# Splitting the product with C in a selective scan between VectorE and GpSimd, in two batches of four

## The chip, the cores and the metric

The kernel runs on one core of one Trainium2 chip. The time is the device time of one execution in microseconds (us): 928.15 us is the median of three runs of the kernel before (926.04, 928.15 and 931.03). Smaller is better.

## The reference, cut to what matters

Two decoder layers run over x (4 batches, 256 tokens, 256 features). The change lies in the first block of the second layer, a selective scan with 512 inner features and 16 states:

```python
def step(h, inputs):              # over the 256 tokens
    dA_t, dBu_t, C_t = inputs
    h = h * dA_t + dBu_t
    y = jnp.einsum('bdn,bn->bd', h, C_t)
    return (h, y)
```

dA is exp(delta * A), dBu is delta * B * u, and y sums, over the 16 states, the state times its value of C at that token. Around it stand, in each batch, linear attention, cross attention and a mixture of experts (layer 0), and after it a cross attention with 32 heads and a second mixture of experts (layer 1).

## The kernel before, in words

**Tiles.** Features lie on the 128 partitions and tokens along the row. A step n of the scan (n from 0 to 15) holds two of the four feature tiles (i = 0, 1) and two states (s = 0, 1), so its state is 128 x 2 x 512 numbers: for each i a half of 512, made of two quarters of 256 tokens, one for each s. The states of five steps lie in a ring (`state(n)`). In the first and the last batch (`alone(b)`) steps 0 to 7 take feature tiles 0 and 1 with all 16 states, and steps 8 to 15 tiles 2 and 3. The middle batches go through the steps in another order.

**One step.** GpSimd multiplies delta*u by B into the state's place (`scan_input`, L603, two steps ahead). ScalarE writes exp(delta*A) into the PSUM banks F[0] and F[1] (`scan_decay`, L846), each after the scan of the step before has read that bank. VectorE runs two scans of 512 (L1606), one for each i. TensorE copies the row of C to all partitions in the PSUM bank F[2] (`spread_c`, two bf16 matmuls against `bcp` and `pick`), after VectorE's product of the step before has read that bank. VectorE multiplies the whole state by F[2] (L1616, 128x1024; in the last step two products of 512, L1613). TensorE adds the quarters into a PSUM bank for y by matmuls with the identity (`sum_states`, L1011). For an even step it adds all four quarters. For an odd step below 15 GpSimd first adds the two quarters of each half (`pair_sum`, L613), and TensorE adds the two results (`parts = 1`). The trace counts each fp32 matmul as two instructions.

**Order.** Every engine is a queue that runs in the order written. The order is a fixed merge of two streams of phases, F (layer 0 and the scan) and B (layer 1 after the scan), by the tables `FILL` and `LATER`. Phase `s{n}` holds step n. In batch 0 its scan (from 138.5 us to 213.9 us) is interleaved with the cross attention and the layer 0 experts of batch 1; in batch 3 (673.4 us to 757.2 us) with the 32-head attention and then the layer 1 experts of batch 2. Inside phase `s{n}` TensorE does `spread_c(n)`, then `sum_states(n-2)`; GpSimd does `scan_input(n+2)`, then the sum of quarters of n-1 if that is odd; ScalarE does `scan_decay(n+1)`; VectorE does scans and product of n. Between them come the other stream's phases: ScalarE's Silu of layer 0 experts (L788), with a load of its table before and another load before the next exponential, its exponentials of the attention (L887) and its Tanh of layer 1 experts (L908); VectorE's L1540, L1693, L1745 and L1751.

The functions that the change touches:

Of the kernel before, what the change touches and what calls it, by code (L numbers as in the profile page):

```python
# [19 lines left out]
ALU = mybir.AluOpType  # L20
# [3 lines left out]
P = 128  # L24
B, S, D = 4, 256, 256
# [10 lines left out]
NSTEP = 2 * NK  # L36
# [188 lines left out]
def build(nc, ins, out, known):  # L225
    ctx = ExitStack()
    with ctx:  # L227
        def sb(name, shape, dt=F32):
            return ctx.enter_context(nc.sbuf_tensor(name, shape, dt))
# [76 lines left out]

        cs = du[:, :, :].rearrange("p d t -> p (d t)")[:, 0:C_END]
        bcp = sb("bcp", [P, S], BF16)

        arena = sb("arena", [P, 8192 + 2560])  # L310
        A_RING = 8
# [41 lines left out]
        F = [banks_f[:, 512 * i:512 * i + 512] for i in range(4)]  # L353
# [5 lines left out]
        def place(b):  # L359
            return places[b]  # L360
# [22 lines left out]
        pf, af, df, gf, pb, ab, db, gb = (steps[n] for n in names)  # L383
# [29 lines left out]
        def head(n):  # L413

            q, j = divmod(n, 4)
            return 8 * (q // 2) + 2 * j + q % 2
# [22 lines left out]

            return NK * dp + NK - 1 if alone(b) else NSTEP - 2 + dp  # L440

        def in_halves(n):

            return n % 2 == 1 and n < NSTEP - 1

        def state(n):

            r = n % RING
            if r == 4:
                return hb5  # L450
            return hb[:, r, :, :]
# [14 lines left out]
        def later(b):  # L466
            return b > 0

        def alone(b):
            return b in (0, B - 1)  # L470
# [84 lines left out]
        def _(pool):  # L555
            g = nc.gpsimd
# [24 lines left out]
            def rsqrt(dst, src, wait, steps_, name):  # L581
                pool.wait_ge(*wait)
                g.tensor_tensor(dst, src, minus_half[:, 0:src.shape[-1]], ALU.pow).then_inc(steps_.step(name), 1)  # L583
# [25 lines left out]
            def pair_sum(b, n):  # L609

                pool.wait_ge(*df.at(f"hc{n}", b))
                h = state(n)
                g.tensor_tensor(h[:, :, 0:S], h[:, :, 0:S], h[:, :, S:2 * S], ALU.add)\  # L613
                    .then_inc(gf.step(f"half{n}"), 1)
# [31 lines left out]
            def front(b, ph):  # L646
                pl = place(b)
                if ph in PAIRS:
                    n = 2 * PAIRS.index(ph) + 1
                    h = head(n)  # L650
                    if n in (1, 9) and not later(b):
                        pool.wait_ge(init_v, 2 if n == 1 else 5)
                    pool.wait_ge(*af.at(f"c{n}", b))
                    a_ = pl.att[:, n % A_RING, :]
                    g.tensor_tensor(a_[:, 0:S], a_[:, 0:S], decay[:, h, :], ALU.mult).then_inc(gf.step(), 1)  # L655
                    g.tensor_tensor(a_[:, S:S + P], a_[:, S:S + P], decay[:, h, 0:P], ALU.mult)\
                        .then_inc(gf.step(f"a{n}"), 1)
                if ph == "ob":
                    rsqrt(rs[:, :], ve[:, :], df.at("ve_o", b), gf, "rs_o")
                    rsqrt(rs[:, :], ve[:, :], df.at("ve_ln1", b), gf, "rs_ln1")  # L660
                if ph == "xc":
                    rsqrt(rs[:, :], ve[:, :], df.at("ve_sim", b), gf, "rs_sim")
                if ph == "xd":
                    rsqrt(rs[:, :], ve[:, :], df.at("ve_ln2", b), gf, "rs_ln2")
                if ph == "fd3":
                    rsqrt(rs3[:, :], ve3[:, :], df.at("ve_ln3", b), gf, "rs_ln3")
                if ph == "m3" and not later(b):
                    prepare(b, gf)
                if ph == "d4":
                    scan_input(b, 0)  # L670
                    scan_input(b, 1)
                if ph in STEPS:
                    n = STEPS.index(ph)
                    if n + 2 < NSTEP:
                        scan_input(b, n + 2)
                    if n >= 1 and in_halves(n - 1):
                        pair_sum(b, n - 1)
                if ph == "u2":
                    rsqrt(rsu[:, :], veu[:, :], df.at("ve_ln4", b), gf, "rs_ln4")

# [31 lines left out]
        def _(act):  # L712
# [122 lines left out]
            def scan_decay(b, n):  # L835

                k, dp = part(b, n)
                if k == 0:
                    act.wait_ge(*af.at(f"delta{dp}", b))
                for i in range(2):  # L840
                    if n >= 1:
                        act.wait_ge(*df.at(f"scan{n - 1}_{i}", b))
                    d = 2 * dp + i
                    for s in range(2):
                        j = d * NS + 2 * k + s
                        ins_ = a.activation(two(F[i][:, :])[:, s, 1:S], delta[:, d, 1:S], ACT.Exp, scale=a_neg[:, j:j + 1])  # L846
                    ins_.then_inc(af.step(f"dA{n}_{i}"), 1)

            def back(b, ph):
                bk = home(b)  # L850
# [64 lines left out]
        def _(pe):  # L915
# [68 lines left out]
            def sum_states(b, n):  # L984

                k, dp = part(b, n)
                if n == 0:
                    pe.wait_ge(*af.at("delta0", b))
                if n == 0 and not alone(b):
                    pe.wait_ge(*db.at("x4_read", b - 1))  # L990
                if n < NSTEP - 1:
                    pe.wait_ge(*(gf.at(f"half{n}", b) if in_halves(n) else df.at(f"hc{n}", b)))
                parts = 1 if in_halves(n) else 2
                if alone(b) and n == NK:
                    pe.wait_ge(*df.at("y_read0", b))
                if n < NTURN and not alone(b):
                    for t in range(TT):
                        for i in range(2):
                            for s in range(parts):
                                c, d = s * S + t * P, (2 * dp + i) * P  # L1000
                                last = t_.matmul(y_bank(b, t)[:, d:d + P], state(n)[:, i, c:c + P], ident[:, :],
                                                 start=(n == 0 and i == 0 and s == 0),
                                                 stop=(n >= NTURN - 2 and s == parts - 1),
                                                 is_transpose=True, skip_group_check=True)
                    last.then_inc(pf.step(f"y{n}"), 1)
                    return
                for i in range(2):
                    if n == NSTEP - 1:
                        pe.wait_ge(*df.at(f"hc{n}_{i}", b))
                    for s in range(parts):  # L1010
                        last = mm(y_bank(b, dp)[:, i * S:i * S + S], ident[:, :], state(n)[:, i, s * S:s * S + S],  # L1011
                                  alone(b) and k == 0 and i == 0 and s == 0, k == NK - 1 and s == parts - 1)
                last.then_inc(pf.step(f"y{n}"), 1)
# [345 lines left out]
        def _(dve):  # L1359
            v = nc.vector  # L1360
# [67 lines left out]
            def front(b, ph):  # L1428
# [12 lines left out]
                if ph in PAIRS:  # L1441
                    n = 2 * PAIRS.index(ph)
                    h = head(n)
# [119 lines left out]
                if ph == "m4":  # L1563

                    for i in range(2):
                        dve.wait_ge(*af.at(f"tap{i}", b))
                        for j in range(1, NCONV):
                            if j > 1:
                                own(df, b)
                            for d in (2 * i, 2 * i + 1):  # L1570
                                c, w = acc[:, S * d + j:S * d + S], V_CW + 4 * d + NCONV - 1 - j
# [24 lines left out]
                if ph in STEPS:  # L1596
                    n = STEPS.index(ph)
                    for i in range(2):
                        h = state(n)[:, i, :]
                        dve.wait_ge(*af.at(f"dA{n}_{i}", b))  # L1600
                        if n == 0:
                            dve.wait_ge(*df.at("first", b))
                            dve.wait_ge(*gf.at(f"dbu0_{i}", b))
                        elif i == 0:
                            dve.wait_ge(*gf.at(f"dbu{n}", b))
                        v.tensor_tensor_scan(h, F[i][:, :], h, 0.0, ALU.mult, ALU.add)\  # L1606
                            .then_inc(df.step(f"scan{n}_{i}"), 1)
                    dve.wait_ge(*pf.at(f"c{n if alone(b) else n - n % 2}", b))
                    own(df, b)
                    h = state(n)  # L1610
                    if n == NSTEP - 1:
                        for i in range(2):
                            v.tensor_tensor(h[:, i, :], h[:, i, :], F[2][:, :], ALU.mult)\  # L1613
                                .then_inc(df.step(f"hc{n}_{i}"), 1)
                    else:
                        v.tensor_tensor(h, h, F[2][:, :].unsqueeze(1).to_broadcast([P, 2, 2 * S]), ALU.mult)\  # L1616
                            .then_inc(df.step(f"hc{n}"), 1)
                    if alone(b) and n == NK + 1:
                        gated_output(b, 0)
# [250 lines left out]
```

## Time and profile before

| what | us |
|---|---|
| median of 3 runs | 928.15 |
| lowest, highest | 926.04, 931.03 |
| the profiled execution, its own time | 930.76 |
| its span in the trace | 929.0 |
| TensorE busy | 840.1 |
| VectorE busy | 636.2 |
| ScalarE busy | 368.0 |
| GpSimd busy | 349.4 |

The profile is of one execution. A group of rows gives, for one line of the kernel, the busy time in all and the mean time of one instruction. PE is the matmul, PEld the weight load beside it, DVE is VectorE, ACT is ScalarE, POOL is GpSimd. A span of time is told in us from the span's start. The granted clock of TensorE is a share of full speed (2.4 GHz), 0.5 being the lower level (1.2 GHz).

### The profile page before, as it was taken

Reading aid. Unit: us, or ns where it says so; the run is one execution under the profiler, and the core shown is the slowest. Engines: PE = TensorE matmul, PEld = TensorE weight load, DVE = VectorE, ACT = ScalarE, POOL = GpSimd, SP = SyncE. Lnnn points to the kernel's source line nnn. Section 1 sums busy time; section 2 is a strip of 40 time slices with the busy share of each in tenths; the row PEclk is TensorE's granted clock in tenths of the full one; section 3 lists DMA queues with packets and bytes.
Section 4 is the critical chain, followed back from the end, with each engine's and each line's share of the span. In section 5 each row is a group of like instructions: output and inputs, shape, how many; then the busy total and the mean of one; then the engine's idle time right before and its main releaser. Section 6 shows DMA issues by size and latency. Waiting matters only on the chain. (4 is left out here: it accounts for less than half of the span.)

```text
span 929.0 us, 12411 instructions
## 1 busy us (share of the span) xinstructions
PE 840.1 (90%) x4566; PEld 632.2 (68%) x4590; DVE 636.2 (68%) x1218; ACT 368.0 (40%) x741; POOL 349.4 (38%) x337
## 2 busy tenths in 40 slices
PE   6889986878988999997989999998697999999996
PEld 5677765647635778886636888876134888738885
DVE  5342479898946278998955469998989886625222
ACT  5121365752254354442263354445385323171110
POOL 4300446651303038781301229861547622102221
PEclk9999998999988999999999999999789899999999
DMA  7202050022030054441020044432100124313442
GB/s 232 93 21 83 11 195 1 0 86 102 1 114 1 22 173 152 135 138 46 2 113 1 7 153 139 135 102 84 56 1 1 40 68 132 103 35 123 161 142 74
DMA packets 26927, 76.10 MB, mean 82 GB/s; under 512 B 3436, under 2 KB 5420, under 8 KB 26228
## 3 DMA queue, kind: packets, MB, share of 16 engines
q1 hardware_dynamic: 26612, 75.26, 24.5%
q8 instruction: 36, 0.59, 0.3%
q14 instruction: 23, 0.19, 0.1%
q10 hardware_dynamic: 256, 0.07, 0.0%
HBM read 74.13 MB, written 1.11 MB: 81 GB/s over the span
## 5 line engine op out<-in xcount | busy, mean ns | idle before, releaser
L919 PE MATMUL B<-late 128*128 128x256 f32 (+2 forms) x1064 | 243.5, 382 | 2.0 <-POOL late L702 1.5
L919 PEld LDWEIGHTS B<-late 128*128 128x128 f32 (+1 forms) x1064 | 199.2, 193 | 32.9 <-POOL late L702 3.2
L603 POOL TENSOR_TENSOR arena<-du,arena 128x1024 f32<-128x1024 f32 x60 | 141.0, 2362 | 30.9 <-PE F L919 30.4
L1606 DVE TENSOR_TENSOR_SCAN arena<-F,arena 128x512 f32<-128x512 f32 x128 | 149.2, 1207 | 2.9 <-ACT F L846 2.8
L846 ACT ACTIVATE F<-delta,a_neg 128x255 f32<-128x255 f32 x256 | 109.6, 468 | 67.3 <-DVE arena L1606 66.8
L702 POOL TENSOR_TENSOR late<-late 128x512 f32<-128x512 f32 x42 | 53.5, 1274 | 136.0 <-DVE late L1751 105.7
L1616 DVE TENSOR_TENSOR arena<-arena,F 128x1024 f32<-128x1024 f32 x60 | 73.3, 1221 | 8.7 <-PE F L919 3.0
L583 POOL TENSOR_TENSOR rs<-ve,minus_half 128x2 f32<-128x2 f32 (+1 forms) x20 | 15.3, 764 | 162.6 <-DVE ve L1556 71.8
L887 ACT ACTIVATE late<-B 128x512 f32<-128x512 f32 x96 | 51.9, 593 | 23.1 <-PE B L919 18.1
L1682 DVE TENSOR_REDUCE nmx<-B 128x4 f32<-128x1024 f32 x48 | 56.6, 1220 | 3.5 <-PE B L919 3.3
L908 ACT ACTIVATE late<-B 128x512 f32<-128x512 f32 x42 | 24.9, 592 | 85.6 <-PE B L919 84.0
L919 PE MATMUL F<-arena,ident 128*128 128x256 f32 x232 | 57.8, 390 | 0.1
L724 ACT ACTIVATE arena<-F 128x384 f32<-128x384 f32 (+6 forms) x44 | 22.2, 508 | 64.1 <-PE F L919 45.2
L919 PEld LDWEIGHTS F<-arena,ident 128*128 128x128 f32 x232 | 43.3, 198 | 5.9 <-DVE arena L1613 0.5
L919 PE MATMUL F<-arena 128*128 128x256 f32 (+1 forms) x204 | 40.0, 343 | 6.7 <-DVE arena L1439 6.1
L919 PEld LDWEIGHTS F<-arena 128*128 128x128 f32 (+1 forms) x204 | 34.6, 196 | 14.0 <-DVE arena L1439 6.8
L613 POOL TENSOR_TENSOR arena<-arena 128x512 f32<-128x512 f32 x28 | 35.9, 1282 | 19.1 <-DVE arena L1616 19.1
L655 POOL TENSOR_TENSOR arena<-arena,decay 128x256 f32<-128x256 f32 x24 | 18.8, 783 | 58.4 <-ACT arena L724 58.1
L1745 DVE SCALAR_TENSOR_TENSOR late<-late,B 128x512 f32<-128x512 f32 x42 | 28.7, 683 | 16.7 <-ACT late L908 16.0
L919 PE MATMUL B<-late,k_t 128*128 128x512 bf16 x85 | 31.0, 416 | 8.3 <-ACT late L887 5.8
L702 POOL TENSOR_TENSOR late<-arena 128x512 f32<-128x512 f32 x14 | 17.8, 1268 | 50.2 <-DVE arena L1751 44.2
L919 PE MATMUL B<-k_t,late 128*128 128x512 bf16 x89 | 28.5, 419 | 8.4 <-DVE nmx L1682 4.9
(359 smaller groups left out, 1470.2 us busy)
## 6 DMA issues: line engine op xcount, KB each, us to landing
late<-in_w_moe SPq DMA_DIRECT2D x112, 384.0 KB, 3.4
room<-in_w_f SPq DMA_DIRECT2D x4, 2544.0 KB, 9.1
arena<-b_out SPq DMA_DIRECT2D x32, 256.0 KB, 5.5
room<-in_w_l SPq DMA_DIRECT2D x4, 768.0 KB, 6.5
w_m<-in_w_m SPq DMA_DIRECT2D x1, 2112.0 KB
room<-in_w_l SPq DMA_DIRECT2D x4, 512.0 KB, 4.3
x_t<-in_x_t SPq DMA_DIRECT2D x4, 256.0 KB, 2.6
x_tok<-in_x_tok SPq DMA_DIRECT2D x4, 256.0 KB, 5.5
```

The source lines that it names most:

```text
L603: g.tensor_tensor(state(n).rearrange("p d (s t) -> p d s t", s=2), du[:, 2 * dp:2 * dp + 2, :].unsqueeze(2).to_broadcast([P, 2, 2, S]), b_ ...
L613: g.tensor_tensor(h[:, :, 0:S], h[:, :, 0:S], h[:, :, S:2 * S], ALU.add)\
L702: g.tensor_tensor(hid1[:, s:s + 2, :], pair_ring(b, p).rearrange("p (u t) -> p u t", u=2), bk.crs[:, int(2 * p >= MTE), :].unsqueeze(1).to ...
L724: a.activation(dst, src, ACT.Copy, **kw).then_inc(steps_.step(name), 1)
L846: ins_ = a.activation(two(F[i][:, :])[:, s, 1:S], delta[:, d, 1:S], ACT.Exp, scale=a_neg[:, j:j + 1])
L887: a.activation(probs[:, m % 4, :], bk.K[m % 2][:, :], ACT.Exp).then_inc(ab.step(f"p{m}"), 1)
L908: a.activation(pair_ring(b, p), pair_banks(b, p)[0][:, :], ACT.Tanh, scale=0.5)\
L919: return t_.matmul(dst, lhsT, rhs, start=start, stop=stop, skip_group_check=True)
L1606: v.tensor_tensor_scan(h, F[i][:, :], h, 0.0, ALU.mult, ALU.add)\
L1616: v.tensor_tensor(h, h, F[2][:, :].unsqueeze(1).to_broadcast([P, 2, 2 * S]), ALU.mult)\
L1682: v.tensor_reduce(nmx[:, s, g // 4, :, j:j + 2].rearrange("p v i -> p i v"), max_banks(b, n), AX_X, ALU.max, negate=True).then_inc(db.step ...
L1745: v.scalar_tensor_tensor(th, th, 1.0, gates[:, :], ALU.add, ALU.mult)\
```

## The change

In the first and last batch, for the odd steps 1 to 13 (seven in each of the two batches): ScalarE copies F[2] to a new tile `c_copy` in SBUF (128x512) right after it has issued the exponentials of that step. VectorE waits for this copy and multiplies only the half i = 0 by F[2]. GpSimd multiplies the half i = 1 by `c_copy`, after the second scan of the step, in the place in its queue where it had added quarters. TensorE waits for both and adds all four quarters. The middle batches are as they were.

```diff
+        c_copy = sb("c_copy", [P, 2 * S])
...
-        def in_halves(n):
-            return n % 2 == 1 and n < NSTEP - 1
+        def in_halves(b, n):
+            return n % 2 == 1 and n < NSTEP - 1 and not alone(b)
+        def split(b, n):
+            return n % 2 == 1 and n < NSTEP - 1 and alone(b)
...
-                    if n >= 1 and in_halves(n - 1):
+                    if n >= 1 and in_halves(b, n - 1):
                         pair_sum(b, n - 1)
+                    if n >= 1 and split(b, n - 1):
+                        pool.wait_ge(*df.at(f"scan{n - 1}_1", b))
+                        pool.wait_ge(*af.at(f"cc{n - 1}", b))
+                        h = state(n - 1)[:, 1, :]
+                        g.tensor_tensor(h, h, c_copy[:, :], ALU.mult).then_inc(gf.step(f"hp{n - 1}"), 1)
...
                     ins_.then_inc(af.step(f"dA{n}_{i}"), 1)
+                if split(b, n):
+                    act.wait_ge(*pf.at(f"c{n}", b))
+                    if n >= 2:
+                        act.wait_ge(*gf.at(f"hp{n - 2}", b))
+                    copy(c_copy[:, :], F[2][:, :], af, f"cc{n}")
...
-                    pe.wait_ge(*(gf.at(f"half{n}", b) if in_halves(n) else df.at(f"hc{n}", b)))
-                parts = 1 if in_halves(n) else 2
+                    pe.wait_ge(*(gf.at(f"half{n}", b) if in_halves(b, n) else df.at(f"hc{n}", b)))
+                if split(b, n):
+                    pe.wait_ge(*gf.at(f"hp{n}", b))
+                parts = 1 if in_halves(b, n) else 2
...
+                    elif split(b, n):
+                        dve.wait_ge(*af.at(f"cc{n}", b))
+                        v.tensor_tensor(h[:, 0, :], h[:, 0, :], F[2][:, :], ALU.mult).then_inc(df.step(f"hc{n}"), 1)
```

## Rows read from the trace of the kernel before

**Rows 1.** The page, part 1: busy us, share of the span, instructions.
```profile
PE 840.1 (90%) x4566; PEld 632.2 (68%) x4590; DVE 636.2 (68%) x1218; ACT 368.0 (40%) x741; POOL 349.4 (38%) x337
```
**Rows 2.** By stretch: length; PE, PEld, DVE, ACT, POOL busy (instructions); granted clock; DMA.
```profile
138.50:213.90 75.40, 58.50 (x243) 43.77 (x242) 70.72 (x90) 42.68 (x82) 43.75 (x23) 0.91 0.08 27
157.35:164.82 7.47, 6.89 (x34) 5.46 (x33) 7.26 (x8) 6.51 (x13) 6.29 (x4) 1.00 0.01 2
673.40:717.00 43.60, 36.18 (x244) 17.88 (x248) 39.42 (x53) 30.30 (x67) 23.78 (x17) 0.93 0.00 1
717.00:757.20 40.20, 39.75 (x178) 34.01 (x179) 36.05 (x55) 14.62 (x37) 22.69 (x25) 0.89 0.19 60
757.20:916.90 159.70, 158.22 (x848) 122.93 (x854) 72.47 (x143) 39.24 (x72) 31.28 (x26) 1.00 0.35 111
```
**Rows 3.** Groups by shape, 717 to 757.2: count, busy us, mean ns, idle before.
```profile
L1616 DVE TENSOR_TENSOR arena<-arena,F 128x1024 f32<-128x1024 f32 x6 | 7.3, 1222 | 1.6 <-PE F L919 1.1
...
L1613 DVE TENSOR_TENSOR arena<-arena,F 128x512 f32<-128x512 f32 x2 | 1.3, 685 | 0.1
...
L724 ACT ACTIVATE late<-B 128x512 f32<-128x512 f32 x2 | 1.2, 597 | 8.3 <-PE B L930 8.0 <-PE B L919 0.3
```
**Rows 4.** Timeline, batch 0, sums of quarters: start, length, what, idle before.
```profile
157.39 1.03 PE L919 MATMUL F<-arena,ident 128*128 128x256 f32 x4
...
162.17 1.89 PE L919 MATMUL F<-arena,ident 128*128 128x256 f32 x8
```
**Rows 5.** Timeline, batch 0, around the start of step 5's scans.
```profile
163.59 1.67 ACT L846 ACTIVATE F<-delta,a_neg 128x255 f32<-128x255 f32 x4
...
164.64 0.39 PE L919 MATMUL F<-bcp,pick 128*128 128x256 bf16 x2 [0.58 <-DVE arena L1616]
...
164.82 2.33 DVE L1606 TENSOR_TENSOR_SCAN arena<-F,arena 128x512 f32<-128x512 f32 x2
...
166.08 0.87 ACT L846 ACTIVATE F<-delta,a_neg 128x255 f32<-128x255 f32 x2 [0.81 <-DVE arena L1606]
```
**Rows 6.** Timeline of VectorE, batch 0, between steps 7 and 8.
```profile
178.04 0.42 DVE L1540 TENSOR_TENSOR late<-late,B 128x256 f32<-128x256 f32 x1 [2.08 <-ACT late L788]
```
**Rows 7.** Timeline of VectorE: the same two products, at two places.
```profile
186.67 2.52 DVE L1649 TENSOR_TENSOR arena<-arena,sres 128x256 f32<-128x256 f32 x2
...
214.76 0.76 DVE L1649 TENSOR_TENSOR arena<-arena,sres 128x256 f32<-128x256 f32 x2
```
**Rows 8.** Timeline of GpSimd, batch 0, beside the first of these.
```profile
182.83 4.67 POOL L603 TENSOR_TENSOR arena<-du,arena 128x1024 f32<-128x1024 f32 x2 [5.32 <-PE F L919]
187.46 1.45 POOL L613 TENSOR_TENSOR arena<-arena 128x512 f32<-128x512 f32 x1
```
**Rows 9.** Timeline of TensorE, batch 0, behind step 13's sum of 11.
```profile
204.67 1.13 PE L919 MATMUL B<-w_lb,late 72*128 72x256 f32 x4 [1.95 <-ACT late L724]
```
**Rows 10.** Timeline, batch 3, steps 3 and 4, beside the attention of batch 2.
```profile
687.94 2.23 ACT L887 ACTIVATE late<-B 128x512 f32<-128x512 f32 x4
...
688.67 0.79 PE L919 MATMUL B<-late,k_t 128*128 128x512 bf16 x2
...
690.05 1.67 ACT L846 ACTIVATE F<-delta,a_neg 128x255 f32<-128x255 f32 x4
...
691.17 1.21 DVE L1606 TENSOR_TENSOR_SCAN arena<-F,arena 128x512 f32<-128x512 f32 x1
```
**Rows 11.** Timeline, batch 3, step 11, beside the experts of batch 2.
```profile
735.81 0.87 ACT L846 ACTIVATE F<-delta,a_neg 128x255 f32<-128x255 f32 x2 [1.65 <-DVE arena L1606]
...
737.57 0.38 PE L919 MATMUL F<-bcp,pick 128*128 128x256 bf16 x2
...
737.77 0.60 ACT L908 ACTIVATE late<-B 128x512 f32<-128x512 f32 x1
...
737.99 1.22 DVE L1616 TENSOR_TENSOR arena<-arena,F 128x1024 f32<-128x1024 f32 x1 [1.10 <-PE F L919]
...
740.58 0.69 DVE L1751 TENSOR_TENSOR late<-late,B 128x512 f32<-128x512 f32 x1 [0.77 <-PE B L919]
```

## The prediction

> **What bounds the kernel now.** I read the busy line of the page first, then the busy time of each engine in five stretches, then the timelines around single steps. There TensorE stands at 90% of the span and VectorE at 68% [rows 1]: TensorE is the engine that is short on the whole. The change acts in two stretches only, so what counts is what is short there [rows 2]. In batch 0's scan (75.4 us) VectorE is busy 70.7 us and TensorE 58.5: VectorE is the bound, with TensorE idle 17 us. In the first part of batch 3's scan, beside the attention of batch 2 (43.6 us), VectorE has 39.4 and TensorE 36.2. In the second part, beside the experts (40.2 us), TensorE has 39.75: it is the bound, and behind it to the end it has 158.2 of 159.7 us. So a microsecond of TensorE's work added there has no gap to vanish in, and one saved on VectorE there is worth nothing by itself.
>
> **The prices.** For each of the 14 odd steps:
> - VectorE: a product of 1024 (1.22 us) becomes one of 512 (0.685) [rows 3]: -0.54, in all -7.5 us.
> - TensorE: an odd sum of four instructions (1.03 us) becomes one of eight (1.89) [rows 4]: +0.86, in all +12.0 us.
> - ScalarE: a copy of 128x512 from PSUM to SBUF, which the trace shows at 0.597 us [rows 3]: +0.60, in all +8.4 us, and the wait for `c{n}` before it.
> - GpSimd: a product of 128x512 out of SBUF in the place of a sum of the same size (L613, 1.45 us) [rows 8]: 0. The bound from the other side: L603 multiplies twice as many in 2.34 us [rows 8], 1.17 for this size, -0.3 us a step. No one waits for GpSimd in these stretches, since the sum on TensorE stands a phase later.
>
> So it takes 7.5 us from VectorE and gives 12.0 to TensorE. Now where each falls.
>
> **Batch 0, steps 1 to 7 (beside the layer 0 experts of batch 1).** A pair of steps lasts 7.47 us, VectorE has 7.26 of it and TensorE 6.89 [rows 2]. With 0.86 more TensorE has 7.75: it becomes the bound, and the pair grows by 0.28. TensorE's present wait for the product, 0.58 us [rows 5], is smaller than what is added. Two pairs are filled like this (steps 3 and 5): +0.6. Step 1 has less of TensorE's work beside it, and VectorE's gain shows in part, since the exponentials of the next odd step are the other limit: in rows 5 the first two of four are done at 163.59 + 0.83 = 164.42, only 0.4 us ahead of the scan at 164.82. I take -0.2. The copy itself is hidden in steps 3 and 5: ScalarE idles 0.81 us behind the exponentials of step 5, and the copy takes 0.60 of it [rows 5]. In step 7 it isn't hidden: two Silus with their table loads come behind it, and VectorE waits 2.08 us for one of them [rows 6]. There +0.6 for the copy and -0.5 for the scan before it, which comes earlier: +0.1. Sum of steps 1 to 7: +0.5 us.
>
> **Batch 0, steps 9 to 13.** Step 9: behind it stand VectorE's two products L1649, which took 2.52 us there and 0.76 us at 214.76 [rows 7]. Beside the long one GpSimd ran without a gap from 182.83 to 188.91 [rows 8], and VectorE's second product ended right behind it. So VectorE waits there for GpSimd's end, which hangs on TensorE's sums (5.32 us of wait), and a product that ends 0.54 earlier only waits longer: 0. Steps 11 and 13: VectorE is dense, TensorE idles up to 1.95 us [rows 9] and takes the 0.86: -0.54 each, -1.1. Batch 0 in all: 0.5 - 1.1 = -0.6 us. Bounds: if every odd step gained, -3.8; if the 0.28 came three times, the copy in step 7 in full, and the two last steps gained nothing, +1.5.
>
> The Trainium skill, "SBUF — State Buffer" (Who interferes with whom), says that a VectorE instruction with two SBUF inputs and a GpSimd instruction that reads SBUF exclude each other for the whole length of the one that came first, while one with a single SBUF input does not contend. The trace agrees: 2.52 us against 0.76 for two SBUF inputs [rows 7, 8]. By that rule the gain of step 9 is lost, as I take it; without it the sum would be 0.54 us lower. And by it the product with F[2], which lies in PSUM, waits for no GpSimd instruction.
>
> **Batch 3, steps 1 to 7 (beside the attention of batch 2).** Here ScalarE has no room. At step 3 the four attention exponentials (687.94, 2.23 us) stand right behind the exponentials of the step, and right behind them those of step 4 (690.05); the scan of step 4 starts at 691.17 [rows 10]. The copy is put ahead of all. With it alone the first two exponentials of step 4 are done at 690.05 + 0.83 + 0.60 = 691.5, so the scan is 0.3 us later than now, and VectorE's gain is a wait. With the longer sum on TensorE, which stands just ahead of the scores at 688.67, these come 0.86 later as well, at 689.5, done by 689.8; two attention exponentials of 0.54 and the two of step 4 (0.83) end at 691.75: 0.6 us later. I take a value between, 0.47, for each of the steps 1, 3, 5 and 7: +1.9 us. Bounds: -0.54 x 4 = -2.2 if the slack is larger than it looks; +0.86 x 4 = +3.4 if TensorE's addition goes in whole.
>
> **Batch 3, steps 9 to 13 (beside the experts).** TensorE idles 0.45 us in 40.2 [rows 2]. Three sums of 0.86: +2.6 us. VectorE's savings buy nothing: at step 11 it already waits 1.10 us for C and 0.77 us for the experts' matmuls [rows 11]. Bounds: +2.1 with the idle time used up, and 0 if the clock gives something back.
>
> **Sum.** -0.6 + 1.9 + 2.6 = +3.9 us. Against the profiled execution (span 929.0, time 930.76) that is 934.7. The median of the runs shown is 2.6 us below it, 928.15, and gives 932.0, +0.4%. Bounds of the terms added: -6.0 + 0 and +1.5 + 3.4 + 2.6 = +7.5, that is 922 to 936.
>
> **The rivals.** About 0.5% (4.6 us) is what a measurement of this kernel can tell from no change: faster is below 923.5, slower above 932.8.
>
> 1. *VectorE is the bound in both stretches (faster).* For it: 70.7 of 75.4 and 39.4 of 43.6 us busy [rows 2]; where TensorE seems full its matmuls may be spread by waits that the trace doesn't show as idle. Then each product gives 0.54: -7.5 us, 920.6. It decides from the point where TensorE's added 0.86 fits in the time that it waits for VectorE; rows 5 show 0.58 us a pair, too little, and from 717 on there is none.
> 2. *ScalarE's wait for C blocks what stands behind it (slower).* The copy waits for `c{n}`, which TensorE issues in the next phase. At step 11 C is there at 737.95 [rows 11]; the copy ends at 738.55, and the exponentials of step 12, done at 735.81 to 737.8 now, come behind it (1.74 us), and the Tanh of the experts ends at 740.9 in place of 738.4: 2.5 us late. VectorE's expert products then end at about 742.3 in place of 741.3, +1.0. My sum counts this as hidden by TensorE's own delay. If it isn't, at steps 11 and 13 that is +2, and if in the attention copy and sum both go in whole (0.60 + 0.86 a step, +5.8 in place of +1.9), the time is 928.15 - 0.6 + 5.8 + 2.6 + 2 = 938. Against it: VectorE waits for C and for matmuls at step 11 as it is.
> 3. *Nothing moves.* The added matmuls fill waits in batch 3's first part, and later idle stretches shrink, so that the granted clock (0.91 and 0.93 in the scan stretches, 1.00 at the end [rows 2]) is better. 0.91 over 75.4 us means 13.6 us at the lower of the two levels, 1.2 GHz; if a quarter of that went, TensorE's work in it would take half the time, -1.7 us, and the added 1.9 of the attention part would be gone with it. Sum about +0.3: 928.5. That is also the rival that the change doesn't do what it says: it moves half a product, and the chain of the step stays.
>
> **How the numbers follow.** My forecast, with a centre of 932.0 and its own range 928.5 to 935.5, gets 0.58; rival 1 gets 0.13, rival 2 0.17, rival 3 0.12. Of the forecast's range 0.26 lies above 932.8. Slower 0.26 + 0.17 = 0.43; faster 0.12 of rival 1's 0.13; same the rest, 0.45. The range, 923 to 937.5, holds the forecast, rival 3 and half of rival 2, and leaves out most of rival 1.
>
> **What would show it.** Product L1616 in two forms, 14 of them at 0.69 us in place of 1.22; L613 left only in the middle batches; TensorE's sums in the two stretches in eights. In batch 0, from 138.5 to 213.9, a stretch within 1 us of 75.4, with VectorE waiting for TensorE's C or for ScalarE at steps 3 to 9. In batch 3, 43.6 us growing to 45.5 and 40.2 to 42.8, TensorE's busy time up by 12 in all, and from 757 to the end no change. ScalarE with waits for `c{n}` of 1 us and more at steps 7 and 11. I am wrong if batch 0's stretch shrinks by over 2 us or the experts' part grows by less than 1.5.

## The result and the profile after

The changed kernel takes 939.01 us (median of 4 runs, 937.34 to 940.57) against 929.38 us for the kernel before in the same comparison: 1.0104 times, 95% interval 1.0072 to 1.0136. Timed once more beside other kernels it was 1.0109 (1.0084 to 1.0135). So it is slower by some 10 us. Forecast were 932.0 us, +3.9 against the baseline, in a range up to 937.5: the direction is right, and the loss is more than twice as large.

The stretches of the profiled execution of the changed kernel, cut at the same instructions as [rows 2] (columns as there):

```profile
139.07:215.57 76.50, 63.82 (x271) 49.55 (x271) 68.00 (x90) 46.73 (x89) 43.87 (x23) 0.92 0.07 26
675.11:720.90 45.79, 39.40 (x260) 20.93 (x264) 37.86 (x54) 32.92 (x72) 23.74 (x17) 0.95 0.01 1
720.90:766.67 45.77, 41.52 (x190) 35.45 (x191) 36.49 (x55) 15.48 (x39) 22.66 (x25) 0.93 0.16 52
766.67:926.37 159.70, 158.16 (x848) 122.94 (x854) 72.42 (x142) 39.25 (x72) 31.25 (x26) 1.00 0.35 111
```

Batch 0's scan lasts 76.50 us in place of 75.40 (+1.1), the part of batch 3 beside the attention 45.79 in place of 43.60 (+2.2), the part beside the experts 45.77 in place of 40.20 (+5.6), and the end is the same to the hundredth, 159.70. The start lies 0.6 us later, and between the two scans nothing changes. Together these make the 9.4 us between the two spans (929.0 and 938.4). TensorE's busy time is up by 11.1 us (840.1 to 851.2), where 12.0 were forecast.

The prices were as forecast. Line numbers of the changed kernel stand a little later than before: L608, L1623 and L934 are L603, L1606 and L919 of the kernel before, L798, L1557 and L1669 are L788, L1540 and L1649, and L1765 is L1745; L734 with `c_copy` is the copy of C, L1634 VectorE's half product and L687 GpSimd's. The kernels of the experiments shift them by a line or two more. The groups of the changed kernel by shape (count, busy us, mean ns, idle before and who ended it):

```profile
L687 POOL TENSOR_TENSOR arena<-arena,c_copy 128x512 f32<-128x512 f32 x14 | 18.0, 1282 | 13.3 <-DVE arena L1623 13.3
...
L1634 DVE TENSOR_TENSOR arena<-arena,F 128x512 f32<-128x512 f32 x14 | 9.6, 689 | 3.2 <-ACT c_copy L734 2.0
L734 ACT ACTIVATE c_copy<-F 128x512 f32<-128x512 f32 x14 | 8.3, 594 | 14.5 <-PE F L934 14.5
```

The half product takes 0.689 us, the copy 0.594, GpSimd's product 1.282. Behind the last bar stands what the prediction had named but given no value: ScalarE stood idle for 14.5 us before its 14 copies, waiting for C.

**Batch 0, step 7.** The timeline of ScalarE in the kernel before showed the exponentials of step 7 ending at 171.63 and the table load of the next Silu right behind; TensorE's timeline shows C of step 7:

```profile
170.76 0.87 ACT L846 ACTIVATE F<-delta,a_neg 128x255 f32<-128x255 f32 x2 [0.24 <-DVE arena L1606]
171.65 1.28 ACT L788 ACT_TABLE_LOAD   x1
```
```profile
172.11 0.39 PE L919 MATMUL F<-bcp,pick 128*128 128x256 bf16 x2 [0.57 <-DVE arena L1616]
```

In the changed kernel, the timelines of all engines, steps 7 to 9:

```profile
170.70 0.87 ACT L856 ACTIVATE F<-delta,a_neg 128x255 f32<-128x255 f32 x2 [0.24 <-DVE arena L1623]
173.38 0.60 ACT L734 ACTIVATE c_copy<-F 128x512 f32<-128x512 f32 x1 [1.80 <-PE F L934]
173.99 1.28 ACT L798 ACT_TABLE_LOAD   x1
...
180.38 0.42 DVE L1557 TENSOR_TENSOR late<-late,B 128x256 f32<-128x256 f32 x1 [4.25 <-ACT late L798]
...
184.43 0.39 PE L934 MATMUL F<-bcp,pick 128*128 128x256 bf16 x2 [3.21 <-DVE arena L1636]
184.66 3.15 PE L934 MATMUL F<-arena,ident 128*128 128x256 f32 x8
...
188.76 3.18 DVE L1669 TENSOR_TENSOR arena<-arena,sres 128x256 f32<-128x256 f32 x2
```

ScalarE is done with its exponentials at 171.57, waits 1.80 us for C, copies, and only then loads the table for the Silus. The 1.80 us have three parts. By the rows of the kernel before, C would be there 0.87 us after the exponentials (172.50 against 171.63). Counted from the first scan, the exponentials now end 0.63 us earlier: VectorE's gain of the steps before did arrive, but it only lengthens the wait. And C comes 0.28 us later. For the load that follows, -0.63 + 1.80 + 0.60 is 1.77 us, and by just that the scan of step 8 is late.

VectorE's wait for the second Silu, 2.08 us before [rows 6], is 4.25 now. TensorE, behind VectorE, waits 3.21 us, and its next eight instructions take 3.15 us in place of 1.89: the lower clock (0.57 granted on average over them). GpSimd's products behind that sum come later, and the two products L1669 that must wait for them take 3.18 us in place of 2.52 [rows 7].

**Batch 3, beside the experts.** TensorE in the kernel before:

```profile
721.32 6.09 PE L919 MATMUL B<-late 128*128 128x256 f32 x16
```

The timelines of the changed kernel from the end of the attention:

```profile
721.03 1.12 PE L945 MATMUL B<-ident,late 128*128 128x128 f32 x4 [3.82 <-DVE late L1425]
...
724.84 3.70 PE L934 MATMUL B<-late 128*128 128x256 f32 x16
728.38 0.38 PE L934 MATMUL F<-bcp,pick 128*128 128x256 bf16 x2
728.60 1.89 PE L934 MATMUL F<-arena,ident 128*128 128x256 f32 x8
734.30 3.45 PE L934 MATMUL B<-late 128*128 128x256 f32 x8 [3.81 <-DVE late L1765]
```
```profile
725.80 2.35 POOL L608 TENSOR_TENSOR arena<-du,arena 128x1024 f32<-128x1024 f32 x1
728.11 1.26 POOL L687 TENSOR_TENSOR arena<-arena,c_copy 128x512 f32<-128x512 f32 x1
730.57 2.34 POOL L608 TENSOR_TENSOR arena<-du,arena 128x1024 f32<-128x1024 f32 x1 [1.20 <-PE F L934]
```
```profile
726.61 1.56 DVE L1738 TENSOR_SCALAR cb<-smb 128x2 f32<-128x2 f32 x1
728.21 1.33 DVE L1742 TENSOR_SCALAR pr<-pr,smb 128x16 f32<-128x16 f32 x2
...
730.96 1.98 DVE L1751 TENSOR_SCALAR smb<-smb 128x2 f32<-128x2 f32 x1
```

In the kernel before TensorE ran the 16 expert instructions there in 6.09 us (granted clock 0.60) and then had no wait over 0.31 us up to step 11. Here they take 3.70 us (granted 1.00): the clock came back earlier, and so did the sum behind them (728.60). GpSimd's product L608 waited for that sum, begins at 730.57 and falls upon VectorE's chain of small instructions for the router. One of them, on 128x2 numbers, which takes 0.17 us alone, lasts 1.98 us, until GpSimd is done. TensorE waits 3.81 us for the end of the chain and runs its next eight instructions at the lower clock, 3.45 us. The gain of 2.4 us by the earlier clock, less 3.8 and 1.6, leaves a loss of 3.0. The three longer sums are the other 2.6: the distribution of C (`spread_c`) stands 6.89 us later than before at step 11, 7.75 at steps 12 and 13, 8.61 at 14 and 15, each step of 0.86 one sum.

### The profile page after: what moved, and what is told of

Same layout as the page of the kernel before. It is cut to its first block and busy times, and to the rows that moved or that the text cites. A ratio compares the mean times of both kernels' runs of the same rounds, so it can differ in the third digit from the quotient of the medians.

```text
span 938.4 us, 12577 instructions
## 1 busy us (share of the span) xinstructions
PE 851.2 (91%) x4622; PEld 643.5 (69%) x4646; DVE 632.5 (67%) x1218; ACT 375.6 (40%) x755; POOL 349.4 (37%) x337
## 5 line engine op out<-in xcount | busy, mean ns | idle before, releaser
L934 PE MATMUL B<-late 128*128 128x256 f32 (+2 forms) x1064 | 242.4, 381 | 5.8 <-DVE late L1765 3.8
L934 PEld LDWEIGHTS B<-late 128*128 128x128 f32 (+1 forms) x1064 | 198.1, 192 | 36.5 <-DVE late L1765 4.2
L608 POOL TENSOR_TENSOR arena<-du,arena 128x1024 f32<-128x1024 f32 x60 | 140.9, 2358 | 35.8 <-PE F L934 33.3
L1623 DVE TENSOR_TENSOR_SCAN arena<-F,arena 128x512 f32<-128x512 f32 x128 | 149.2, 1207 | 5.1 <-ACT F L856 4.9
L934 PE MATMUL F<-arena,ident 128*128 128x256 f32 x288 | 70.6, 391 | 0.0
L1636 DVE TENSOR_TENSOR arena<-arena,F 128x1024 f32<-128x1024 f32 x46 | 56.2, 1222 | 8.7 <-PE F L934 4.4
L934 PEld LDWEIGHTS F<-arena,ident 128*128 128x128 f32 x288 | 54.2, 197 | 6.9
L734 ACT ACTIVATE arena<-F 128x384 f32<-128x384 f32 (+6 forms) x44 | 22.2, 508 | 64.1 <-PE F L934 45.2
L934 PE MATMUL F<-arena 128*128 128x256 f32 (+1 forms) x204 | 40.0, 343 | 6.7 <-DVE arena L1456 6.1
L934 PEld LDWEIGHTS F<-arena 128*128 128x128 f32 (+1 forms) x204 | 34.6, 196 | 14.0 <-DVE arena L1456 6.8
L1765 DVE SCALAR_TENSOR_TENSOR late<-late,B 128x512 f32<-128x512 f32 x42 | 28.7, 683 | 19.0 <-ACT late L923 18.4
L934 PE MATMUL B<-late,k_t 128*128 128x512 bf16 x85 | 31.0, 416 | 8.7 <-ACT late L902 6.2
L934 PE MATMUL B<-k_t,late 128*128 128x512 bf16 x89 | 28.5, 419 | 8.4 <-DVE nmx L1702 4.9
L1242 PE MATMUL B<-late,v 128*32 128x256 f32 x384 | 33.7, 416 | 0.0
```

The source lines that it names most:

```text
L608: g.tensor_tensor(state(n).rearrange("p d (s t) -> p d s t", s=2), du[:, 2 * dp:2 * dp + 2, :].unsqueeze(2).to_broadcast([P, 2, 2, S]), b_ ...
L734: a.activation(dst, src, ACT.Copy, **kw).then_inc(steps_.step(name), 1)
L934: return t_.matmul(dst, lhsT, rhs, start=start, stop=stop, skip_group_check=True)
L1242: last = t_.matmul(bk.K[2 + g % 2][32 * j:32 * j + 32, 0:S], v32[:, t, g, :], probs[:, m % 4, i * S:i * S + S], start=(t == 0), stop=(t == ...
L1765: v.scalar_tensor_tensor(th, th, 1.0, gates[:, :], ALU.add, ALU.mult)\
```

## The experiments

Each was timed against the kernel before on the same chip. Offsets of scans are the start of a scan after the first scan of batch 0, less the same in the profiled execution of the kernel before.

| kernel | ratio to before, 95% interval | scan of step 8, batch 0 | first scan of batch 3 | added from there to the scan of step 9 |
|---|---|---|---|---|
| changed | 1.0104 (1.0072 to 1.0136) | +1.77 | +1.12 | +2.2 |
| e5, changed again | 1.0109 (1.0084 to 1.0135) | +1.77 | +1.09 | +2.2 |
| e1, sums only | 1.0030 (1.0014 to 1.0047) | +0.11 | -2.41 | +1.6 |
| e2, copy only | 1.0017 (0.9993 to 1.0041) | +1.49 | +0.66 | +1.4 |
| e3, changed, router first | 1.0067 (1.0043 to 1.0091) | +1.79 | +0.47 | +2.6 |
| e4, changed, step 7 whole | 1.0043 (1.0021 to 1.0064) | -0.06 | -3.05 | +2.6 |
| e6, batch 0 without step 7 | 0.9988 (0.9967 to 1.0010) | -0.06 | -2.52 | -0.3 |
| e7, batch 0, all steps | 1.0037 (1.0016 to 1.0057) | +2.28 | +0.92 | -0.3 |
| e8, batch 3, all steps | 1.0055 (1.0032 to 1.0078) | 0.00 | -2.31 | +2.4 |
| e9, before, router first | 1.0003 (0.9977 to 1.0028) | +0.01 | -4.66 | 0.0 |
| e10, e6 and router first | 0.9986 (0.9969 to 1.0002) | -0.06 | -3.21 | -0.3 |
| e11, e8 and router first | 1.0052 (1.0024 to 1.0080) | 0.00 | -3.15 | +2.8 |
| e12, step 7 of batch 0 alone | 1.0020 (1.0000 to 1.0041) | +1.50 | -1.43 | 0.0 |
| e13, GpSimd sums | 1.0015 (0.9990 to 1.0039) | -1.09 | -4.76 | -0.3 |
| e14, experts' steps alone | 1.0045 (1.0021 to 1.0069) | +0.01 | -0.16 | 0.0 |

First a warning that these columns gave. In e8, e9, e11 and e14 batch 0 is the kernel before, instruction by instruction; yet their batch 3 begins 2.31, 4.66, 3.15 and 0.16 us earlier than in the profile of before. That profile was one draw among several: executions of the same instructions differ. One place where the draws part is seen in the timeline of TensorE in e8, which answers to "176.01 3.22" of the kernel before:

```profile
176.54 1.99 PE L935 MATMUL B<-xt,room 128*128 128x256 f32 x8 [1.78 <-DVE late L1558]
```

The wait before it is the same 1.78 us; in the kernel before the eight instructions behind it then ran in 3.22 us, the lower clock, and here in 1.99. Of the five traces in which batch 0 is unchanged, two show the lower clock there (before, and e14 with 3.31 us) and three don't (e8, e9, e11, 1.99 each). So an offset of a few us in a trace speaks of a cause only where the instruction rows beside it show it; the ratio over many runs decides on the size.

**e1, sums only.** The sum of quarters by GpSimd goes in both batches, TensorE does it; nothing else.
```diff
-            return n % 2 == 1 and n < NSTEP - 1
+            return n % 2 == 1 and n < NSTEP - 1 and not alone(b)
```


> Only one part of the change: in the first and last batch TensorE sums all four quarters of odd steps too; VectorE keeps the whole product, ScalarE copies nothing, GpSimd adds nothing there. Theory (three causes: ScalarE's copy behind its wait for C in batch 0, TensorE's longer sums, and in batch 3 a collision of VectorE's router chain with GpSimd): the sums alone cost at most 0.6 us in batch 0, 1 to 2 us in batch 3 beside the attention, 2.6 us beside the experts; +4.5 us over before (3 to 6), plus up to 4 if the router chain happens to meet GpSimd here as well. Rival A (TensorE's added 12 us of work explain the whole loss): +9 us or more. Rival B (ScalarE's wait for C explains the loss): +0 to +2 us.

+2.8 us (1.3 to 4.4 by the interval), under the +4.5 expected. Rival A falls: all of TensorE's 12 us of added work cost less than a third of the loss, less than half by the upper bound. In the trace batch 0 takes it without harm, +0.11 at step 8.

**e2, copy only.**
```diff
+                if split(b, n):
+                    act.wait_ge(*pf.at(f"c{n}", b))
+                    copy(c_copy[:, :], F[2][:, :], af, f"cc{n}")
...
+                        if split(b, n):
+                            dve.wait_ge(*af.at(f"cc{n}", b))
                         v.tensor_tensor(h, h, F[2][:, :].unsqueeze(1).to_broadcast([P, 2, 2 * S]), ALU.mult)\
```


> Only the other part: the kernel before with ScalarE's copy of C in the odd steps of the first and last batch, and VectorE's wait for it; nobody reads the copy, VectorE keeps the whole product and GpSimd adds the quarters. Theory: +2 us at step 8 of batch 0 (the Silu chain behind step 7's copy is late), +1 to +1.5 us beside the attention, 0 beside the experts where TensorE is the bound; in all +3 to +4 us. Rival A (TensorE's added work explains the loss): 0. Rival B (ScalarE's wait for C explains the loss): +6 us or more, most of it beside the experts.

The scan of step 8 comes 1.49 us late with the copy alone, and 1.4 us are lost beside the attention, as the theory has it; beside the experts nothing moves (+2.06 at step 9 of batch 3, +2.07 at steps 10 and 11), against rival B, save 0.7 at step 12. ScalarE's wait for C at step 7 is 0.91 us here, near the 0.87 that the rows of before give, and 0.91 + 0.60 is the lateness of step 8. The time, +1.6 us (-0.7 to 3.8), can't be told from rival A's 0, nor from the +3 expected.

**e3, changed kernel, GpSimd waits for the router chain in the last batch.**
```diff
+                if n == 12 and b == B - 1:
+                    pool.wait_ge(*db.at("cb1", b - 1))
```


> The changed kernel, but in the last batch GpSimd begins its product for step 12 (128x1024, needed 20 us later) only when VectorE's router chain of batch 2's second expert layer is done. Theory (the chain of small VectorE instructions was held up by GpSimd's long ones, TensorE idled 3.8 us for it and then ran 8 instructions at the lower clock in 3.45 us instead of 1.9): the idle time goes, 4 to 5 us faster than the changed kernel, about 934.5. Rival B (the loss beside the experts comes from ScalarE's copies waiting for C at steps 9 and 11): no change against the changed kernel, 939, or slower by GpSimd's delay.

In its trace the router chain runs undisturbed, TensorE's wait is gone, and the scan of step 10 stands at +0.42 in place of +4.79. The ratio is 1.0067 against 1.0104 and 1.0109, so 3 to 4 us less where 4 to 5 were expected; the intervals overlap a little. The trace alone doesn't show what the wait does: its 16 expert instructions took 5.39 us, so the clock came back late in it. In e4's trace they took 5.42 us, without the added wait, and TensorE's wait is down to 0.30 us as well.

**e4, changed kernel, step 7 of batch 0 whole.**
```diff
-            return n % 2 == 1 and n < NSTEP - 1 and alone(b)
+            return n % 2 == 1 and n < NSTEP - 1 and alone(b) and not (b == 0 and n == 7)
```
(ScalarE then waits for the last step that was split before it may write the copy again; so in all split kernels below but e5.)

> The changed kernel without the split in step 7 of batch 0 (VectorE takes the whole product, GpSimd adds the quarters, no copy of C there). Theory (step 7's copy waits 1.8 us for C, and two Silus and VectorE wait behind it): the scan of step 8 starts 1.5 to 2 us earlier after the scan of step 0 than in the changed kernel, and the time is 1.5 us lower, about 937.5. Rival A (TensorE's longer sums of steps 1 to 5 make step 8 late): no change, or 0.3 us.

The scan of step 8 is 1.83 us earlier than in the changed kernel, as expected; the time fell by far more than the 1.5 us expected, 1.0043 against the changed kernel's 1.0109 in e5, some 6 us. That made step 7 the first suspect for the missing part.

**e5, e6, e7, e8.** The changed kernel again, and the split in one batch alone:
```diff
-            return n % 2 == 1 and n < NSTEP - 1 and alone(b)
+            return n % 2 == 1 and n < NSTEP - 1 and b == 0 and n != 7        # e6
+            return n % 2 == 1 and n < NSTEP - 1 and b == 0                   # e7
+            return n % 2 == 1 and n < NSTEP - 1 and b == B - 1               # e8
```


> The changed kernel once more, beside the others of this call. Its four runs so far lay in two groups, 937.4 and 940.5. Theory: the loss beside the experts has a part (some 3 us) that hangs on whether two long GpSimd products fall upon VectorE's router chain, so the runs fall in two groups again, and the ratio to before is 1.008 to 1.010. Rival A (TensorE's added work is the whole cause): one group, at +9 to +10 us.

> Split in batch 0 alone, steps 1, 3, 5, 9, 11, 13; step 7 and batch 3 as before. Theory: in e4 batch 0 came out 2.65 us shorter than before at step 15 and the rest of its loss lay in batch 3; so here about -3 us against before, 0.997. Rival A: TensorE's 5 us of added work cost their time somewhere behind, +2 to +5 us.

> Split in all seven odd steps of batch 0, none in batch 3. Theory: +1.1 us against before, as the changed kernel has at the start of batch 1's scan; 4 us more than with step 7 left whole (1.8 of it the late Silus, 1.9 VectorE's two products at step 9 that wait for GpSimd). Rival A: +6 us, all seven sums in full.

> Split in all seven odd steps of batch 3, none in batch 0. Theory: +2.2 us beside the attention and +2.6 us beside the experts, and 0 to 3 us more by the collision of the router chain with GpSimd: +4.8 to +7.8 us, 1.005 to 1.008. Rival A: +6 us with no spread between runs. Rival B (ScalarE's wait for C): VectorE's waits for the copy beside the experts show as idle time of TensorE behind them.

e5's six runs lie from 938.5 to 943.0 without a gap that would show two groups, so the two groups expected weren't found.

e7 costs 3.4 us (0.0037 of 931; 1.5 to 5.3 by the interval), where +1.1 was expected, and e8 5.1 (3.0 to 7.3), in sum 8.5 of the 10; e6, without step 7, gives 1.1 us with an interval that holds zero. e7 less e6 is 0.0049, 4.6 us for step 7; with the two intervals put together that is some 2 to 7. So by the times batch 0's loss is +3.4 and not the +1.1 that the two traces show. The profile of before stood in a slower draw there, which hides part of it. e6 falls short of the expected 3 us for the same reason: batch 3's first scan is 2.52 us early in it, but 2.31 us early in e8 too, with no split in batch 0 at all.

e7 also showed the router's collision with batch 3 as before. Its timelines there:

```profile
721.45 3.70 PE L935 MATMUL B<-late 128*128 128x256 f32 x16
...
731.36 3.62 PE L935 MATMUL B<-late 128*128 128x256 f32 x8 [4.26 <-DVE late L1766]
```

So batch 3's split isn't needed for it: it follows on the early return of the clock. In the four traces without the added wait in which the 16 instructions took 3.70 us (changed, e5, e7, e8), TensorE waited 3.81 to 4.26 us behind them; in the eight in which they took 5.42 to 6.22 us (before, e1, e2, e4, e6, e12, e13, e14), 0.66 at most. That gave theories C and D for the next three.

**e9, e10, e11.** The wait of e3 in the kernel before, in e6 and in e8.

> The kernel before, with one wait added: in the last batch GpSimd begins its product for step 12 only after VectorE's router chain of batch 2. Theory C (the collision of GpSimd with the router chain is a state of the kernel before as well, entered when TensorE's clock comes back early, and the change is not its cause; e7, with batch 3 left as before, showed it): 1 to 2 us faster in the median, and less spread between runs. Theory D (the change itself causes the collision, the kernel before is free of it): no change.

> e6 (split in batch 0 alone, steps 1, 3, 5, 9, 11, 13) with the same wait of GpSimd for the router chain in the last batch. Theory C: both gains add, -2.5 us of the split (as e6's trace) and -1 to -2 of the wait: 3.5 to 4.5 us faster than before, 0.996. Theory D: -1 us, as e6 was timed (0.9988).

> e8 (split in all odd steps of batch 3, none in batch 0) with the same wait. What is left is TensorE's longer sums and ScalarE's copies. Theory C: +2.2 us beside the attention and +2.6 beside the experts in the trace, less the 1 to 2 us that the wait gives in the kernel before: +3 to +4 against before, and in the trace no idle stretch of TensorE over 1 us between 723 and 757. Theory D: 3 us less than e8 (+5.1), so +2. Rival B (ScalarE's copies that wait for C beside the experts cost time): more than +5.

All three times are those of the kernels without the wait (1.0003; 0.9986 against 0.9988; 1.0052 against 1.0055). Theory C isn't borne out in size: the collision is real in single traces, but no gain of the wait that takes it away is seen in the median. A gain of up to 2 us, as C had it for e9, lies within the interval; the 0.996 that it gave for e10 does not. e11's interval, 2.2 to 7.4 us, holds C's +3 to +4 and rival B's over +5, and D's +2 lies just outside it. e10's timeline of TensorE shows one reason, the row after the router chain:

```profile
731.27 5.41 PE L937 MATMUL B<-late 128*128 128x256 f32 x16 [2.00 <-POOL late L714]
```

GpSimd, now late with the scan's products, is late with the experts' product (L714), and TensorE waits 2.00 us for that and runs on at the lower clock. e11 less e9 is 0.0049, 4.6 us, beside 2.2 + 2.6 of the sum: batch 3's cost is the part beside the attention and the three sums. Why e3 still seemed better than the changed kernel by 0.004 stays open.

**e12, e13, e14.** Step 7 alone; e6 with GpSimd's sum of quarters kept behind its product; and steps 9, 11 and 13 of batch 3 alone:
```diff
+            return n == 7 and b == 0                                         # e12
+            return n % 2 == 1 and NK < n < NSTEP - 1 and b == B - 1          # e14
...
                         g.tensor_tensor(h, h, c_copy[:, :], ALU.mult).then_inc(gf.step(f"hp{n - 1}"), 1)
+                        pool.wait_ge(*gf.at(f"hp{n - 1}", b))
+                    if n >= 1 and in_halves(b, n - 1):                       # e13: all odd steps
+                        pair_sum(b, n - 1)
```


> The kernel before with one step split, step 7 of batch 0. Theory: ScalarE's copy there waits for C and stands ahead of two Silus and their table loads; VectorE's and then TensorE's wait grow, TensorE's clock falls behind its wait of over 3 us, and VectorE's two products at step 9 meet a later GpSimd block: the whole loss of batch 0 in one step, +3 to +4.5 us, 1.003 to 1.005. Rival A (TensorE's longer sums make batch 0 late): +0 to +0.5 us, since one sum is 0.86 us.

> Split in batch 0, steps 1, 3, 5, 9, 11, 13, but GpSimd adds the quarters of these steps as in the kernel before, behind its product, so that TensorE's work isn't longer. Theory E (in batch 0 VectorE's gain is lost to TensorE's longer sums in steps 3 and 5, 0.3 us each, and elsewhere to ScalarE's exponentials): 0.5 to 1 us better than e6 (0.9988), so -1.5 to -2 us, 0.998. Rival (GpSimd has 2 x 2.36 + 1.28 + 1.28 = 7.3 us of work in a pair of steps that would last 6.9, and becomes the bound): no better than e6, scans of steps 5 to 7 later than in e6.

> The kernel before with steps 9, 11 and 13 of batch 3 split, beside the experts. Theory: TensorE is the bound, so three longer sums of 0.86 us, +2.6 us, 1.003; in the trace VectorE waits at step 11 for the copy, and TensorE doesn't wait behind it. Rival B (the copies that wait for C hold up the experts' Tanh and cost time): +4 us or more. Rival C (VectorE's shorter products give something back): under +1.5.

e12 shows step 7's chain with nothing else changed. The timelines of ScalarE, VectorE and TensorE, as in the changed kernel but for ScalarE's wait, which is half as long:

```profile
173.08 0.60 ACT L734 ACTIVATE c_copy<-F 128x512 f32<-128x512 f32 x1 [0.91 <-PE F L935]
```

```profile
180.07 0.42 DVE L1558 TENSOR_TENSOR late<-late,B 128x256 f32<-128x256 f32 x1 [4.13 <-ACT late L798]
```
```profile
184.13 0.39 PE L935 MATMUL F<-bcp,pick 128*128 128x256 bf16 x2 [3.08 <-DVE arena L1637]
184.36 2.90 PE L935 MATMUL F<-arena,ident 128*128 128x256 f32 x8
```

The scan of step 8 is 1.50 us late. The time is up by 1.9 us (interval 0 to 3.8), less than the 3 to 4.5 expected and more than rival A's 0.5 only in its middle. The three estimates of step 7 (1.9 here, 4.6 from e7 less e6, some 6 from e4 against e5) all point to a loss but not to one size, and e12's interval reaches zero.

In e13 the scans of steps 5 and 7 come 0.62 and 1.00 us earlier than in before, in e6 0.08 earlier and 0.03 later: TensorE's longer sums do eat VectorE's gain in steps 3 and 5. The time doesn't show it (1.0015, where 0.998 was expected and e6 has 0.9988).

e14 costs 4.2 us (2.0 to 6.4). The 2.6 expected lies in the interval, and so does rival B, "+4 us or more", which the median meets; rival C's "under +1.5" doesn't. The trace speaks against rival B. Counted from the first scan of batch 0 it ends 2.5 us later than that of before, as three sums have it, and at step 11 VectorE waits for the copy and TensorE runs on without a wait:

```profile
741.74 0.69 DVE L1635 TENSOR_TENSOR arena<-arena,F 128x512 f32<-128x512 f32 x1 [2.04 <-ACT c_copy L734]
```
```profile
742.54 3.62 PE L935 MATMUL B<-late 128*128 128x256 f32 x16
```

No kernel here is shown to be faster than the one before; e6 and e10 come nearest, and both intervals hold 1.

## Why the prediction was wrong, step by step

**Prices: right.** 0.69, 0.86 and 0.60 us were measured as forecast, and GpSimd's 1.28 lies between its two bounds, 1.17 and 1.45.

**Batch 0, steps 1 to 5: right in size.** -0.2 and +0.6 were forecast; from step 1 to the scan of step 7 the changed kernel stands at +0.03, by way of -0.53 at step 2. From scan 1 to scan 3 it gains 0.33 and from scan 3 to scan 7 loses 0.34. That the longer sums take VectorE's gain is shown by e13.

**Batch 0, step 7: the step that failed.** The prediction said: "There +0.6 for the copy and -0.5 for the scan before it, which comes earlier: +0.1." It priced the copy and left out the wait ahead of it, which it had named as a price of ScalarE in general. The rows needed were in the trace: ScalarE free at 171.63, C of step 7 begun at 172.11 and 0.39 long, so 0.87 us of wait before a copy of 0.60, 1.47 in all, and e12 has +1.50 at the scan of step 8. And the -0.5 couldn't be had, since exponentials that end earlier don't bring C earlier. In the changed kernel the copy waits 1.80 us for C, with two Silus queued behind it. Measured: +1.74 us from the scan of step 7 to that of step 8 and, with what that sets off (TensorE's wait of 3.21 us, the lower clock, the later GpSimd block), 4.6 us between e6 and e7 and 1.9 in e12. So batch 0's term is not -0.6 but +3.4 (e7).

**Batch 0, step 9: half right.** The two products did wait for GpSimd's end, and the gain of 0.54 was lost; but in draws where TensorE's clock holds, as e8's, they wait for less, and the scan of step 10 stands 1.3 us earlier. In the changed kernel the late sum puts them back, +0.7 more.

**Batch 0, steps 11 and 13: right in the trace.** 2.12, 1.58, 1.57, 1.02: -0.54 each.

**Batch 3, attention: right.** +1.9 forecast, +2.2 measured; e1 and e2 show that the sums alone (+1.6) and the copy alone (+1.4) each cost most of it, and they overlap.

**Batch 3, experts: right in the median, wrong in the one trace.** +2.6 for three sums: shown by the steps of 0.86 and by the +2.5 of e14's trace; e14's time, +4.2, leaves room for more. The +5.6 of the profiled execution has 3.0 us more from a clock that came back early and the collision that followed, and e7 has that with batch 3 unchanged. The prediction had no place for it: its "No one waits for GpSimd in these stretches" doesn't hold for VectorE's router chain. With e11 less e9 the whole of batch 3 is 4.6 us against the 4.5 forecast.

**Rival 2 named the mechanism and put it in the wrong place.** It had ScalarE's wait for C stop what stands behind it, but at steps 11 and 13 of batch 3, where TensorE hides it: in e14's trace the Tanh and VectorE's products are late and TensorE doesn't wait for them. It gave 938 by those sums. What it describes happened at step 7 of batch 0.

**The chances.** Of the forecast's 0.58, the prediction put 0.26 above 932.8; an even spread over its range gives 0.22. Nothing else hangs on it.

**The sum with its terms mended:** +3.4 + 4.8 = +8.2 us against 8.5 for e7 and e8 together and 9.6 to 10.2 for both at once. The +3.4 is e7's own time, so this adds up the parts and doesn't test step 7's share. The last 1 to 2 us are within the intervals and not explained.

## What to carry to other kernels

When a step is given a new consumer on another engine, price its wait before its work: read when the operand is ready, when that engine's queue comes to it, and what is queued behind. A copy of 0.6 us, priced at +0.1 in net, cost some 2 to 6 us in the one step of fourteen where it stood right ahead of a table load. And before a trace is read as cause, compare several executions of unchanged code: here identical instructions moved by up to 4.7 us between traces.

## What the runs showed of the hardware

- The same wait of 1.78 us before TensorE was followed by the lower clock in two traces (eight instructions in 3.22 us in before, 3.31 in e14) and not in three others (1.99 us in e8, e9, e11) of the same instruction stream. What decides it isn't seen here.
- A small VectorE instruction can last as long as a GpSimd instruction on 1024 numbers a row: 128x2 in 1.98 us in place of 0.17, and 1.56 in place of 0.15, each until GpSimd's instruction had ended. VectorE's half product with one operand in PSUM took 0.69 us in all 14 steps, in 12 of them with a GpSimd instruction running beside it. The Trainium skill, "SBUF — State Buffer" (Who interferes with whom), has both: a `tensor_scalar` out of SBUF may take the pair of ports that GpSimd uses and is then held until a GpSimd instruction that began first has ended, and an instruction with at most one SBUF input outside such a mode is not held.
- A faster TensorE can lose time within one execution: in the changed kernel's trace it ran 16 instructions 2.4 us faster, released GpSimd earlier, and that stopped the chain that TensorE then waited for, 3.81 us. Taking the collision away showed no gain in the median (e9, 1.0003).
